# Attention over 16 groups: TensorE's program without its hardware loop, two key tiles of the row sums added elsewhere, four output buffers

## The chip, the cores and the metric

The kernel runs on one core of a Trainium2 chip. The metric is the device time of one execution in microseconds (us). Three executions of the kernel before took 3575.22, 3578.84 and 3588.54 us; the median is 3578.84 us. The profile comes from a further execution of its own.

## What is computed

The input x has 2 sequences of 2048 tokens with 1024 features. Cut to what matters:

```python
xn = layernorm(x)
q, k, v = xn @ wq, xn @ wk, xn @ wv      # 32 query heads, 8 key/value heads of 32 features
scores = where(causal, (q . k) * 32 ** -0.5, lowest)
s = (softmax(scores) @ v).reshape(b, s, 1024) @ wo
w = top-2-of-8 router weights of xn
g = silu(xn @ W_base.T + b_base + LoRA mixture of xn by w)
out = x + s * g
```

All operands are float32. The products are made exact enough by splitting a number into a rounded high part and the rest.

## The kernel before

The program has four parts, one after the other: project() makes q, k and v and stores them to DRAM, attend() does the attention, gate() makes g, output() multiplies by wo and finishes. The change touches attend() alone.

**Groups, chunks, tiles.** A group is one sequence with one key/value head and its NREP = 4 query heads; there are NG = 16 groups. A group has CPB = 4 chunks of CH = 512 queries, c = 0 to 3. Chunk c sees 4(c + 1) key tiles of 128 keys, j = 0, 1, .... For a pair of a key tile j and a block i of 128 queries TensorE makes one 128 x 512 tile of scores, keys by (head, query): that is operation T (line 1005, with line 1008 for the mask on the diagonal), 136 for a group, of which 10, 26, 42 and 58 belong to chunks 0 to 3. ScalarE takes the exponential of each (line 1043) into a buffer of 128 x 2048 for the whole key tile. The stretch from the first T of chunk c to the first T of the next chunk is called stage c here, and its start Sc.

**Row maxima ahead.** The shift for the softmax comes from scores in the other layout, queries by keys: TensorE makes pieces of rows (operation S, line 923, up to 512 keys), VectorE takes their maxima (lines 1067 and 1071), and operation M turns them into a row of the operand of T (lines 929, 1082, 817). These pieces run LEAD = 84 tiles ahead, so that those of the next group stand in this group's stages; four PSUM banks hold them.

**Values.** After each two key tiles of a chunk, operation W multiplies their exponentials by v, four matmuls per key tile (line 961). When the chunk is done, operation O on ScalarE copies the sum to o_sb (line 1057). There are two buffers o_sb, chosen by cc % 2.

**Row sums.** The softmax needs the sum of the exponentials over all keys. Three ways share this, by tables:

```python
ADDS = [[0, 1, 2, 3], [0, 3, 5, 6, 7], [0, 3, 5, 6, 8, 9, 10, 11], [0, 3, 5, 6, 8, 10, 12]]
DMA_ADDS = [[], [1, 2, 4], [1, 2, 4, 7], [1, 2, 4, 7, 9, 11]]
REST = [[], [], [], [13, 14, 15]]
```

The first tile of a list is the accumulator itself (buffers added and dma_added). GpSimd adds the other tiles of ADDS onto it (operation A, line 890). The others of DMA_ADDS are added by accumulating transfers of 1 MB, which GpSimd issues (operation D, line 900), each after the one before has landed. The tiles of REST are kept. Operation Y (line 978) is TensorE's: for each of added, dma_added and the tiles of REST it does four matmuls with a matrix of ones, and so waits until GpSimd's adds and the transfers of the chunk have ended. Y(c) stands nine tiles or so into the next stage; Y(3) in stage 0 of the next group.

**After the sums.** ScalarE copies Y's result to l_sb (line 1050, two buffers). Then L1 (line 860) moves a few rows of it to l_few, VectorE takes the reciprocal (operation I, line 1114), L2 (line 864) stores 8 KB to DRAM, L3 (line 868) spreads it back over l_sb in four transfers, GpSimd multiplies o_sb by l_sb (operation N, line 912), and L4 (line 873) stores o_sb and counts o_stored. L1 to L4 are issued by SyncE, whose queue is in order: L4(c) waits there for N(c).

**What sets the order.** stage(c) writes the operations in one list for all engines, by tile numbers: A(c,j), D(c,j), Y(c), N(c) and so on are the letters used below with chunk and key tile. Each engine goes through the lists in order. ScalarE's program is written out for all groups (over_stages_once, line 736); the others use over_stages (line 714), which has a hardware loop over pairs of groups (line 719), with three stages ahead of it and five behind:

```python
with engine.Fori(0, NPAIR - 1) as pair:
    for c in range(PEEL, CPB):
        run(Step(pair, 0), c, STAGES[c])
```

In both O(c) and Y(c) ScalarE waits for o_stored[cc % 2], that is, until the chunk two back has been multiplied and stored (lines 1049 and 1055). Of the 16 groups, groups 0 to 15, the loop's body goes from stage 3 of an even group to stage 2 of the next even one.

## Time and profile before

| what | value |
|---|---|
| runs | 3575.22, 3578.84, 3588.54 us |
| the profiled execution's own time | 3588.89 us |
| its span | 3587.1 us |
| mean granted TensorE clock | 0.957 |
| TensorE matmuls busy | 3328.6 us (93%) |
| VectorE busy | 1889.7 us (53%) |
| ScalarE busy | 1443.8 us (40%) |
| GpSimd busy | 1371.6 us (38%) |

The span is that from the first instruction to the last of the program; the profiled execution's own time is 1.8 us longer. Attention takes from about 709 to 2805 us of the span. The shares are averages over the four parts; what a wait is worth is read in attention itself. The granted clock is the share of 2.4 GHz at which TensorE ran; 0.50 is 1.2 GHz.

### The profile page before, as it was taken

What the parts mean: (1) busy time and instruction counts of PE and PEld (TensorE: products, weight loads), DVE (VectorE), ACT (ScalarE), POOL (GpSimd) and SP (SyncE); (2) the same over time, 40 slices, a digit from 0 to 9 for tenths busy, and PEclk for the clock granted to TensorE, in tenths of its full rate; (3) what the DMA queues carried; (4) which work ended last, traced back from release to release, by engine and by line L of the source; (5) the groups of instructions that cost most, each with busy time, mean ns of one, the idle gap of its engine ahead of it and who ended that gap; (6) DMA issues with size and microseconds to landing.
All of it is one profiled execution on the core that took longest, in us unless ns stands there. A gap on an engine that the chain in (4) does not pass through costs nothing. (4 is left out here: it accounts for less than half of the span.)

```text
span 3587.1 us, 59110 instructions
## 1 busy us (share of the span) xinstructions
PE 3328.6 (93%) x17920; PEld 2219.9 (62%) x17920; DVE 1889.7 (53%) x4622; ACT 1443.8 (40%) x2658; POOL 1371.6 (38%) x565
## 2 busy tenths in 40 slices
PE   6999999799989988989999998999999699999999
PEld 5888888554545544544554554554554488877887
DVE  5333332676666666766766666676673222223333
ACT  3122121165655555655655555565565210100100
POOL 0000000075665665766766675676577100000000
PEclk9999999699999999999999999999999899999999
DMA  6555544356556556656656655655565454435554
GB/s 223 160 163 180 160 153 135 89 125 130 128 122 135 126 119 138 135 122 133 141 119 136 135 125 121 139 130 121 130 153 130 138 172 137 133 126 190 193 190 172
DMA packets 285847, 511.84 MB, mean 143 GB/s; under 512 B 41120, under 2 KB 156832, under 8 KB 263584
## 3 DMA queue, kind: packets, MB, share of 16 engines
q1 hardware_dynamic: 260256, 333.04, 31.5%
q0 software_dynamic: 23040, 167.78, 23.2%
q10 hardware_dynamic: 2304, 7.87, 0.6%
q8 instruction: 137, 2.24, 0.3%
q14 instruction: 110, 0.90, 0.1%
HBM read 205.03 MB, written 134.74 MB: 95 GB/s over the span
## 5 line engine op out<-in xcount | busy, mean ns | idle before, releaser
L890 POOL TENSOR_TENSOR added<-added,probs 128x2048 f32<-128x2048 f32 (+3 forms) x320 | 1182.5, 3695 | 806.8 <-PE o_ps L961 772.5
L1067 DVE TENSOR_REDUCE row_max<-rows_ps 128x1 f32<-128x512 f32 x1536 | 996.3, 683 | 417.6 <-PE rows_ps L923 415.9
L1043 ACT ACTIVATE probs<-cols_ps 128x512 f32<-128x512 f32 x1728 | 921.7, 609 | 324.1 <-PE cols_ps L1005 296.9
L1071 DVE CUSTOM_DVE_ANT_0 masked_rows<-rows_ps,tri 128x128 bf16<-128x128 f32 (+3 forms) x1024 | 485.0, 482 | 228.3 <-PE rows_ps L923 225.3
L1005 PE MATMUL cols_ps<-q_st,k_st 97*128 97x512 f32 x1248 | 530.3, 432 | 54.7 <-ACT dma_added L1043 54.1
L923 PE MATMUL rows_ps<-k_st,q_st 96*128 96x512 f32 (+3 forms) x1536 | 536.5, 382 | 24.7 <-DMA q_st<-scratch_q_hi 16.9
L961 PE MATMUL o_ps<-probs,v_st 128*32 128x512 f32 (+3 forms) x4224 | 434.1, 528 | 0.0
L1005 PE MATMUL cols_ps<-q_st_last,k_st 97*128 97x512 f32 x928 | 388.7, 433 | 34.5 <-issue 30.3
L1005 PEld LDWEIGHTS cols_ps<-q_st,k_st 97*128 97x128 f32 x1248 | 242.0, 194 | 225.6 <-issue 106.9
L923 PE MATMUL rows_ps<-k_st,q_st_last 96*128 96x512 f32 (+3 forms) x1024 | 373.8, 390 | 1.9
L923 PEld LDWEIGHTS rows_ps<-k_st,q_st 96*128 96x128 f32 x1536 | 302.5, 198 | 116.9 <-DVE row_max L1067 49.2
L900 POOL DMA_DIRECT2D dma_added<-probs x160 | 139.9, 875 | 519.6 <-ACT probs L1043 448.0
L1005 PEld LDWEIGHTS cols_ps<-q_st_last,k_st 97*128 97x128 f32 x928 | 177.9, 192 | 188.4 <-issue 124.0
L438 PE MATMUL acc<-xt_hi,w_hi 128*128 128x512 f32 x704 | 281.6, 400 | 1.3 <-DVE logits L381 1.3
L440 PE MATMUL acc<-xt_hi,w_lo 128*128 128x512 f32 x704 | 277.6, 394 | 0.0
L439 PE MATMUL acc<-xt_lo,w_hi 128*128 128x512 f32 x704 | 276.8, 393 | 0.0
L1248 PE MATMUL g_acc<-gw_hi,g_t_hi 128*128 128x512 f32 x576 | 225.2, 391 | 22.0 <-DMA g_t_lo<-scratch_hw_lo 21.8
L961 PEld LDWEIGHTS o_ps<-probs,v_st 128*32 128x32 f32 x4224 | 112.5, 110 | 214.0 <-issue 145.2
L1043 ACT ACTIVATE added<-cols_ps 128x512 f32<-128x512 f32 x256 | 140.5, 598 | 239.0 <-PE cols_ps L1005 151.1
L923 PEld LDWEIGHTS rows_ps<-k_st,q_st_last 96*128 96x128 f32 x1024 | 200.5, 196 | 57.1 <-DVE row_max L1067 22.7
L395 DVE SCALAR_TENSOR_TENSOR out_lo<-acc,out_hi 128x512 fp32r<-128x512 f32 x80 | 55.3, 692 | 324.3 <-ACT out_hi L290 324.3
L1250 PE MATMUL g_acc<-gw_hi,g_t_lo 128*128 128x512 f32 x576 | 224.8, 390 | 0.0
(113 smaller groups left out, 3912.3 us busy)
## 6 DMA issues: line engine op xcount, KB each, us to landing
dma_added<-probs POOLq DMA_DIRECT2D x160, 1024.0 KB, 7.7
q_st<-scratch_q_hi SPq DMA_DIRECT2D x96, 256.0 KB, 6.9
x_sb<-in_x SPq DMA_DIRECT2D x32, 512.0 KB, 4.0
scratch_xt_hi<-xt_hi SPq DMA_DIRECT2D x32, 512.0 KB, 6.1
scratch_xt_lo<-xt_lo SPq DMA_DIRECT2D x32, 512.0 KB, 6.8
scratch_q_hi<-out_hi SPq DMA_DIRECT2D x64, 256.0 KB, 2.4
scratch_q_lo<-out_lo SPq DMA_DIRECT2D x64, 256.0 KB, 2.9
l_sb<-scratch_l_inv SPq DMA_DIRECT2D x256, 64.0 KB, 5.0
```

The costliest lines, as they stand in the source:

```text
L438: nc.tensor.matmul(out, lh, rh, start=(k == 0), stop=False)
L439: nc.tensor.matmul(out, lh, rl, start=False, stop=False)
L440: ins = nc.tensor.matmul(out, ll, rh, start=False, stop=(k == KT - 1))
L890: nc.gpsimd.tensor_tensor(total[:, :, q0:CH], total[:, :, q0:CH], probs_of(c, j)[:, :, q0:CH], ALU.add).then_inc(pool_added, 1)
L923: nc.tensor.matmul(rows_ps[rows_slot(k)][:, 0:keys], q_st[c][0:K1, h, i * P:(i + 1) * P], k_st[kbuf][0:K1, CH * p:CH * p + keys], start=Tr ...
L961: ins = nc.tensor.matmul(o_ps[h * HD:(h + 1) * HD, q0:CH], v_st[vbuf][:, j, :], probs_of(cc, j)[:, h, q0:CH], start=(j == 0), stop=(j == s ...
L1005: ins = nc.tensor.matmul(into, k_st[n.u][:, j * P:(j + 1) * P], q_st[c][:, :, i * P:(i + 1) * P], start=True, stop=not diagonal)
L1043: nc.scalar.activation(probs_of(c, j)[:, :, i * P:(i + 1) * P], cols_ps[cols_slot(AT_T[t])][:, :].rearrange("p (h q) -> p h q", h=NREP), A ...
L1067: nc.vector.tensor_reduce(into, bank[:, :], AX.X, ALU.max).then_inc(rows_free, 1)
L1071: nc.vector.tensor_tensor_reduce(masked_rows[rows_slot(k)][:, 0:keys], bank[:, 0:keys], tri[:, CH - keys:CH], 1.0, MASKED, ALU.add, ALU.ma ...
L1248: nc.tensor.matmul(acc[half][:, :], t_hi[u][:, k, :], w_hi[:, k, cols], start=(k == 0), stop=False)
L1250: return nc.tensor.matmul(acc[half][:, :], t_lo[u][:, k, :], w_hi[:, k, cols], start=False, stop=(k == NW - 1))
```

## The change

Three things are done.

- TensorE's attention program goes through over_stages_once, so its hardware loop is gone and all waits have constants. In the last group that function now leaves out the row pieces of a group after it, as over_stages did.
- In chunk 3 key tile 11 goes from the transfers to GpSimd (in the place of tile 12), and key tile 12 goes from GpSimd to REST, so that Y(3) has four matmuls more. DMA_ADDS of chunk 3 then has five tiles: the accumulator and four transfers onto it.
- There are four buffers o_sb and four counts o_stored, one for each chunk. O(c) waits until the same chunk of the group before has been stored. Y(c) waits for norm_ready instead, that is, until GpSimd's multiply of the chunk two back has read l_sb.

```diff
--- before.py
+++ after.py
@@ -544,10 +544,10 @@
 
 
 
-ADDS = [[0, 1, 2, 3], [0, 3, 5, 6, 7], [0, 3, 5, 6, 8, 9, 10, 11], [0, 3, 5, 6, 8, 10, 12]]
-DMA_ADDS = [[], [1, 2, 4], [1, 2, 4, 7], [1, 2, 4, 7, 9, 11]]
-
-REST = [[], [], [], [13, 14, 15]]
+ADDS = [[0, 1, 2, 3], [0, 3, 5, 6, 7], [0, 3, 5, 6, 8, 9, 10, 11], [0, 3, 5, 6, 8, 10, 11]]
+DMA_ADDS = [[], [1, 2, 4], [1, 2, 4, 7], [1, 2, 4, 7, 9]]
+
+REST = [[], [], [], [12, 13, 14, 15]]
 RING = [(c, j) for c in range(CPB) for j in range(TPC * (c + 1)) if j not in ADDS[c][:1] + DMA_ADDS[c][:1]]
 NRG = len(RING)
 
@@ -674,7 +674,7 @@
         masked_rows = [sb(f"masked_rows{i}", [P, CH], BF16) for i in range(NROWS)]
         shift = sb("shift", [P, NREP * TPC], FP32R)
         row = [sb(f"row{i}", [NREP * TPC, P]) for i in range(2)]
-        o_sb = [sb(f"o_sb{i}", [P, CH]) for i in range(2)]
+        o_sb = [sb(f"o_sb{i}", [P, CH]) for i in range(CPB)]
         l_sb = [sb(f"l_sb{i}", [P, CH]) for i in range(2)]
         l_few = [sb(f"l_few{i}", [P, NL]) for i in range(2)]
         l_inv = [sb(f"l_inv{i}", [P, NL]) for i in range(2)]
@@ -704,7 +704,7 @@
         l_inv_stored = [sem(f"a_l_inv_stored{i}") for i in range(2)]
         l_spread = [sem(f"a_l_spread{i}") for i in range(2)]
         norm_ready = sem("a_norm_ready")
-        o_stored = [sem(f"a_o_stored{i}") for i in range(2)]
+        o_stored = [sem(f"a_o_stored{i}") for i in range(CPB)]
         gw_loaded = sem("a_gw_loaded")
         NW = KT + 1
 
@@ -736,7 +736,8 @@
 
             for g in range(NG):
                 for c in range(CPB):
-                    run(Step(g // 2, g % 2), c, [op for op in STAGES[c] if not (g == 0 and of_group_before(op))])
+                    run(Step(g // 2, g % 2), c, [op for op in STAGES[c]
+                                                   if not (g == 0 and of_group_before(op) or g == NG - 1 and of_group_after(op))])
             for c in range(PEEL):
                 run(Step(NPAIR, 0), c, [op for op in STAGES[c] if of_group_before(op)])
 
@@ -871,10 +872,10 @@
                             wait_apart(sp, norm_ready, count, passed)
                             dst = sc["o"].rearrange("b g p c -> (b g) p c")
                             sp.dma_start(dst[bass.ds(n.lin(1, -back), 1), :, cc * CH:(cc + 1) * CH].squeeze(0),
-                                         o_sb[par][:, :]).then_inc(o_stored[par], 16)
+                                         o_sb[cc][:, :]).then_inc(o_stored[cc], 16)
             over_stages(sp, run)
-            for s in range(2):
-                sp.wait_ge(o_stored[s], 16 + 16 * (CPB * NG // 2))
+            for s in range(CPB):
+                sp.wait_ge(o_stored[s], 16 + 16 * NG)
             sp.wait_ge(gw_loaded, 16 * NW)
 
         @block.gpsimd
@@ -909,7 +910,7 @@
                         _, cc, back = op
                         wait_apart(pool, chunk_copied, n.lin(CPB, cc + 1 - CPB * back), passed_pool)
                         wait_apart(pool, l_spread[cc % 2], n.lin(32 * NREP, 16 * NREP * (cc // 2 + 1) - 32 * NREP * back), passed_pool)
-                        nc.gpsimd.tensor_tensor(o_sb[cc % 2][:, :], o_sb[cc % 2][:, :], l_sb[cc % 2][:, :], ALU.mult) \
+                        nc.gpsimd.tensor_tensor(o_sb[cc][:, :], o_sb[cc][:, :], l_sb[cc % 2][:, :], ALU.mult) \
                             .then_inc(norm_ready, 1)
             over_stages(pool, run)
 
@@ -1011,7 +1012,7 @@
                         weigh(n, *op[1:])
                     elif kind == "Y":
                         row_sums(n, *op[1:])
-            over_stages(pe, run)
+            over_stages_once(run)
 
         @block.scalar
         def _(act):
@@ -1046,15 +1047,17 @@
                     elif kind == "Y":
                         cc, back = op[1:3]
                         act.wait_ge(cols_full, cols_count(n, AT_Y[cc]))
-                        act.wait_ge(o_stored[cc % 2], n.lin(32, 16 * (cc // 2) + 16 - 32 * back))
+
+                        if cc >= 2 or not (first_group(n) or n.lin(1, -back) == 0):
+                            act.wait_ge(norm_ready, n.lin(CPB, cc - 1 - CPB * back))
                         nc.scalar.activation(l_sb[cc % 2][:, :], cols_ps[cols_slot(AT_Y[cc])][:, :], ACT.Copy) \
                             .then_inc(probs_ready, 1)
                     elif kind == "O":
                         cc, back = op[1:3]
 
-                        act.wait_ge(o_stored[cc % 2], n.lin(32, 16 * (cc // 2) + 16 - 32 * back))
+                        act.wait_ge(o_stored[cc], n.lin(16, 16 - 16 * back))
                         act.wait_ge(values_done, n.lin(NVG, J_OFF[cc + 1] // PER_VISIT - back * NVG))
-                        nc.scalar.activation(o_sb[cc % 2][:, :], o_ps[:, :], ACT.Copy).then_inc(chunk_copied, 1)
+                        nc.scalar.activation(o_sb[cc][:, :], o_ps[:, :], ACT.Copy).then_inc(chunk_copied, 1)
             over_stages_once(run)
 
         @block.vector
```

How the order moves, at the places that the prediction speaks of.

TensorE, at the end of the loop's body and just behind it (stage 2 turns into stage 3 there), before:

```order
L921 REGISTER_ALU
L923 MATMUL rows_ps<-k_st,q_st 128x384 [waits a_rows_free]
L921 REGISTER_ALU
L923 MATMUL rows_ps<-k_st,q_st 128x512 [waits a_rows_free]
L961 MATMUL o_ps<-probs,v_st 32x512 [waits a_probs_ready]
L961 MATMUL o_ps<-probs,v_st 32x512 x3
L961 MATMUL o_ps<-probs,v_st 32x384 x4
L719 REGISTER_ALU
L719 COMPARE_AND_BRANCH
L1005 MATMUL cols_ps<-q_st_last,k_st 128x512 [waits a_probs_ready,a_row_moved1]
L923 MATMUL rows_ps<-k_st,q_st 128x512 [waits a_rows_free]
L1005 MATMUL cols_ps<-q_st_last,k_st 128x512 [waits a_probs_ready]
```

The same place, between stages 2 and 3 of group 2, after the change:

```order
L924 MATMUL rows_ps<-k_st,q_st 128x384 [waits a_rows_free]
L924 MATMUL rows_ps<-k_st,q_st 128x512 [waits a_rows_free]
L962 MATMUL o_ps<-probs,v_st 32x512 [waits a_probs_ready]
L962 MATMUL o_ps<-probs,v_st 32x512 x3
L962 MATMUL o_ps<-probs,v_st 32x384 x4
L1006 MATMUL cols_ps<-q_st_last,k_st 128x512 [waits a_probs_ready,a_row_moved1]
L924 MATMUL rows_ps<-k_st,q_st 128x512 [waits a_rows_free]
L1006 MATMUL cols_ps<-q_st_last,k_st 128x512 [waits a_probs_ready]
```

The branch and the register operations are gone; the matmuls and their waits stand in the same order.

GpSimd, the end of its work for chunk 3 (the first row is A(3,8)), before:

```order
L890 TENSOR_TENSOR added<-added,probs 128x2048 [waits a_pool_added]
L67 REGISTER_ALU
L67 REGISTER_ALU [waits a_probs_ready]
L900 DMA dma_added<-probs 128x2048 [waits a_dma_done]
L885 REGISTER_ALU
L889 REGISTER_ALU [waits a_probs_ready]
L890 TENSOR_TENSOR added<-added,probs 128x2048 [waits a_pool_added]
L67 REGISTER_ALU
L67 REGISTER_ALU [waits a_probs_ready]
L900 DMA dma_added<-probs 128x2048 [waits a_dma_done]
L885 REGISTER_ALU
L889 REGISTER_ALU [waits a_probs_ready]
L890 TENSOR_TENSOR added<-added,probs 128x2048 [waits a_pool_added]
```

After the change:

```order
L891 TENSOR_TENSOR added<-added,probs 128x2048 [waits a_pool_added]
L67 REGISTER_ALU
L67 REGISTER_ALU [waits a_probs_ready]
L901 DMA dma_added<-probs 128x2048 [waits a_dma_done]
L886 REGISTER_ALU
L890 REGISTER_ALU [waits a_probs_ready]
L891 TENSOR_TENSOR added<-added,probs 128x2048 [waits a_pool_added]
L886 REGISTER_ALU
L890 REGISTER_ALU [waits a_probs_ready]
L891 TENSOR_TENSOR added<-added,probs 128x2048 [waits a_pool_added]
```

A(3,8), D(3,9), A(3,10), D(3,11), A(3,12) has become A(3,8), D(3,9), A(3,10), A(3,11).

ScalarE, O(3) (o_sb) and Y(3) (l_sb) of group 0, which stand in stage 0 of group 1, before:

```order
L1043 ACTIVATE added<-cols_ps 128x4x128 [waits a_cols_full] x4
L1043 ACTIVATE probs<-cols_ps 128x4x128 [waits a_pool_added,a_values_done,a_cols_full]
L1057 ACTIVATE o_sb<-o_ps 128x512 [waits a_values_done,a_o_stored1]
L1043 ACTIVATE probs<-cols_ps 128x4x128 [waits a_cols_full] x2
L1043 ACTIVATE probs<-cols_ps 128x4x128 [waits a_pool_added,a_values_done,a_cols_full]
L1043 ACTIVATE probs<-cols_ps 128x4x128 [waits a_cols_full]
L1043 ACTIVATE probs<-cols_ps 128x4x128 [waits a_dma_done,a_values_done,a_cols_full]
L1050 ACTIVATE l_sb<-cols_ps 128x512 [waits a_o_stored1,a_cols_full]
```

After the change:

```order
L1044 ACTIVATE added<-cols_ps 128x4x128 [waits a_cols_full] x4
L1044 ACTIVATE probs<-cols_ps 128x4x128 [waits a_pool_added,a_values_done,a_cols_full]
L1060 ACTIVATE o_sb<-o_ps 128x512 [waits a_values_done,a_o_stored3]
L1044 ACTIVATE probs<-cols_ps 128x4x128 [waits a_cols_full] x2
L1044 ACTIVATE probs<-cols_ps 128x4x128 [waits a_pool_added,a_values_done,a_cols_full]
L1044 ACTIVATE probs<-cols_ps 128x4x128 [waits a_cols_full]
L1044 ACTIVATE probs<-cols_ps 128x4x128 [waits a_dma_done,a_values_done,a_cols_full]
L1053 ACTIVATE l_sb<-cols_ps 128x512 [waits a_norm_ready,a_cols_full]
```

The rows stand where they stood. The copy to o_sb waits for the count of chunk 3 alone, where o_stored1 counted chunks 1 and 3 together, and the copy to l_sb for the multiply instead of a store. For O(1) both programs name o_stored1, but only in the first does it count chunk 3 too.

## Rows read from the trace of the kernel before

**Rows 1.** The page: engines, and TensorE's instruction fetches (packets, MB, share).

```profile
PE 3328.6 (93%) x17920; PEld 2219.9 (62%) x17920; DVE 1889.7 (53%) x4622; ACT 1443.8 (40%) x2658; POOL 1371.6 (38%) x565
...
q8 instruction: 137, 2.24, 0.3%
```

**Rows 2.** Waits of PE, 700 to 2900 us: us in total, times, longest.

```profile
PE cols_ps L1005 <- ACT dma_added L1043: 57.2, 31, 4.5
PE cols_ps L978 <- DMA dma_added<-probs: 55.6, 13, 5.4
PE cols_ps L1005 <- issue: 30.3, 6, 5.3
```

**Rows 3.** Timeline of PE: start, us, instruction [idle before it <- releaser].

```profile
1005.20 0.80 PE L1005 MATMUL cols_ps<-q_st,k_st 97*128 97x512 f32 x1 [3.55 <-ACT dma_added L1043]
...
1043.64 0.79 PE L1005 MATMUL cols_ps<-q_st_last,k_st 97*128 97x512 f32 x1 [4.93 <-issue]
...
1107.17 1.08 PE L978 MATMUL cols_ps<-added,ones 128*32 128x512 f32 x4 [4.58 <-DMA dma_added<-probs]
```

**Rows 4.** Stretches right behind waits: us, busy of each engine, PEclk, DMA share.

```profile
1005.20:1011.50 6.30, 6.30 (x26) 2.75 (x30) 1.95 (x4) 2.62 (x5) 1.06 (x1) 0.50 0.52 124
...
1107.20:1110.50 3.30, 3.30 (x16) 0.76 (x20) 0.00 (x0) 0.00 (x0) 2.69 (x2) 0.50 0.93 187
...
2755.80:2759.10 3.30, 3.30 (x15) 1.06 (x7) 0.00 (x0) 0.96 (x2) 0.00 (x0) 0.50 0.02 5
```

**Rows 5.** Timeline of PE, group 0: starts of stages 2, 3, Y(2), next group.

```profile
740.67 0.50 PE L1005 MATMUL cols_ps<-q_st,k_st 97*128 97x512 f32 x1
...
776.23 0.50 PE L1005 MATMUL cols_ps<-q_st_last,k_st 97*128 97x512 f32 x1
...
786.84 1.06 PE L978 MATMUL cols_ps<-added,ones 128*32 128x512 f32 x8 [1.90 <-POOL added L890]
...
825.97 0.50 PE L1005 MATMUL cols_ps<-q_st,k_st 97*128 97x512 f32 x1
```

**Rows 6.** Timeline of PE: starts of stages 0, 1 and 2 of group 3.

```profile
1093.69 0.50 PE L1005 MATMUL cols_ps<-q_st,k_st 97*128 97x512 f32 x1
...
1111.95 0.50 PE L1005 MATMUL cols_ps<-q_st,k_st 97*128 97x512 f32 x1
...
1133.51 0.50 PE L1005 MATMUL cols_ps<-q_st,k_st 97*128 97x512 f32 x1
```

**Rows 7.** Timeline of PE, group 15: its start, Y(2), Y(3).

```profile
2670.17 0.50 PE L1005 MATMUL cols_ps<-q_st,k_st 97*128 97x512 f32 x1
...
2755.01 1.27 PE L978 MATMUL cols_ps<-added,ones 128*32 128x512 f32 x8 [2.82 <-issue]
...
2799.71 1.93 PE L978 MATMUL cols_ps<-added,ones 128*32 128x512 f32 x8 [5.40 <-DMA dma_added<-probs]
```

**Rows 8.** Timeline of POOL, group 0: D(2,4), N(1), A(2,8) to A(2,11), D(3,11), A(3,12).

```profile
761.15 0.87 POOL L900 DMA_DIRECT2D dma_added<-probs  x1 [2.20 <-ACT probs L1043]
...
773.32 1.29 POOL L912 TENSOR_TENSOR o_sb<-o_sb,l_sb 128x512 f32<-128x512 f32 x1 [1.17 <-DMA l_sb<-scratch_l_inv]
774.58 12.13 POOL L890 TENSOR_TENSOR added<-added,probs 128x2048 f32<-128x2048 f32 x4
...
825.95 0.87 POOL L900 DMA_DIRECT2D dma_added<-probs  x1 [1.92 <-DMA dma_added<-probs]
826.56 4.90 POOL L890 TENSOR_TENSOR added<-added,probs 128x2048 f32<-128x2048 f32 x1
```

**Rows 9.** Timeline of POOL, stage 2 of group 3: N(0) and D(2,2).

```profile
1147.84 1.28 POOL L912 TENSOR_TENSOR o_sb<-o_sb,l_sb 128x512 f32<-128x512 f32 x1 [6.75 <-DMA l_sb<-scratch_l_inv]
1152.06 0.87 POOL L900 DMA_DIRECT2D dma_added<-probs  x1 [2.94 <-ACT probs L1043]
```

**Rows 10.** All instructions of line 900, the accumulating transfers of 1 MB.

```profile
DMA to landing us min/median/max: 6.8/7.7/14.0
```

**Rows 11.** Waits of SyncE's DMA queue: us in total, times, longest.

```profile
SPq L68 <- DMA scratch_l_inv<-l_inv: 113.8, 48, 7.2
```

## The prediction

> **What bounds the kernel now.** The page comes first. TensorE is busy 93% of the span, GpSimd 38% [rows 1], but GpSimd's work lies in attention alone. So attention's waits on TensorE are read next. Three releasers hold nearly all of them: a copy on ScalarE (57.2 us), the accumulating transfers in front of Y (55.6 us), and "issue", TensorE waiting for nothing but its own program (30.3 us, 6 times, one for each jump back of a loop with 7 passes) [rows 2]. The timeline shows one of each in groups 2 and 3: 3.55, 4.93 and 4.58 us [rows 3]. The first bears the name of dma_added because T stands behind it in ScalarE's queue, but what ScalarE waits for just ahead is the copy O(1), until o_sb of chunk 3 is stored.
>
> Each wait has an aftermath. Behind the wait of 3.55 us TensorE is granted 0.50 (1.2 GHz instead of 2.4) for 6.3 us with no idle time, behind that of 4.58 us for 3.3 us, and so it is behind one of only 2.82 us [rows 4, 7]. Work done at half the clock takes twice its time, so the aftermath costs half the stretch: 3.1 us behind O(1), about 1.7 behind Y(3); the branch is like the former, taken as 2.7.
>
> I cost the change not wait by wait but by stretches that I put together to a group, since a wait that goes may uncover the next one. The 14 groups 1 to 14 take 2670.17 - 825.97 = 1844.2 us, 131.7 each [rows 5, 7].
>
> **The pieces without the waits.** Stage 1 took 1133.51 - 1111.95 = 21.56 us with no wait inside [rows 6]. Stage 0 took 1111.95 - 1093.69 = 18.26; less its wait of 4.58 and 1.7 for the clock, 12.0 [rows 3, 4, 6]. Stage 2 of group 0 has neither an O(1) that waits nor a branch: 776.23 - 740.67 = 35.56 [rows 5]. From Y(2) to the next group it took 825.97 - 786.84 = 39.13 [rows 5].
>
> **Part 1, the loop goes.** The six waits on issue disappear, with 6 x (4.93 + 2.7) = 46 us at most. Stages 0 to 2 of group 0 and what follows the loop are already written out, and stage 2 there had no such wait [rows 5]; I cost the longer program at nothing. The register operations that go stood beside matmuls; nothing for them either. The page has 137 fetches for 35,840 instructions of TensorE [rows 1], so a block comes for each 262 of them, and the loop fetched its body anew in each pass: the traffic stays.
>
> **Part 2, tiles 11 and 12.** Y(3) gets four matmuls of 512 columns. Eight such took 1.06 us [rows 5], so 0.45 for the four, on TensorE's path, 7 us in all. D(3,11) goes. In group 0 it was issued at 825.95 [rows 8], when the next group began; now the last transfer is D(3,9), which had landed by then, since D(3,11) waited for it. So Y(3)'s last transfer has landed when the next group begins, nine tiles ahead of Y(3), and the wait of 4.58 goes with its 1.7. What is late next there? GpSimd: A(3,11) follows A(3,10) at once and takes 4.9 instead of A(3,12) (826.56 to 831.5 in group 0 [rows 8]). It needs neither tile 12 nor the transfer's issue, so it ends about 5 us sooner, and that was in time. Cost 0. GpSimd's adds stay 20 in number, its issues fall from 10 to 9 of 0.87 us. Tile 12's buffer now comes free at Y(3) only; its next user is key tile 6 of chunk 1, well into stage 1: nothing.
>
> **Part 3, four o_sb.** O(1) waits for a store a whole group old: its 3.55 us and 3.1 go. SyncE's queue is unchanged. Y(1)'s copy gets a wait for N(3), which by the table of events is due at tile 32 and Y(1) at tile 46: nothing, bounded above by the few us that O(1) waited for the same chain, one store further.
>
> **What becomes late: Y(2).** Stage 2 shrinks by 6.6 us, but GpSimd has the same work to do in it, and Y(2) needs A(2,11). In group 0, where O(1) did not wait, Y(2) had to wait 1.90 us for it [rows 5]. Group 0 is the mild case. There N(0) had no N(3) and no L4(3) ahead of it. In group 3 N(0) started at 14.3 us after S2 and ended at 15.6; D(2,2) was then not held up by it, since ScalarE's tile came later still, at 18.6 [rows 9]. With O(1)'s wait gone the tile comes 6.6 us sooner (12 us after S2) and N(0) becomes what holds D(2,2), at 15.6. It lands 6.8 to 7.7 us later [rows 10], so D(2,4) goes out at 23.0. In group 0 it took 774.58 + 12.13 - 761.15 = 25.6 us from D(2,4) to the end of A(2,11), of which 1.17 was a wait for l_sb [rows 8], which here is over before: 24.4. So A(2,11) ends 47.4 us after S2, where TensorE is ready for Y(2) at 786.84 - 1.90 - 740.67 = 44.3 [rows 5]. I forecast a wait of about 3 us at each Y(2), a new bound by GpSimd. The clock: behind 1.90 us no loss (eight matmuls took 1.06 there, the full speed), behind 2.82 half clock for 3.3 us [rows 4, 5]. The new wait is nearer to the second, so I take 1.0 of the 1.7.
>
> **The sum.** A group then takes 12.0 + 0.45 + 21.56 + 47.4 + 39.13 + 1.0 = 121.5 us. 14 groups: 1701, or 143 less. Group 0 had no wait that goes. Group 15: from its start to Y(2) it took 84.84 [rows 7], now 12.45 + 21.56 + 47.4 = 81.4, so 3.4 less; its Y(3) waited 5.40 us for D(3,11) and now waits for A(3,11) instead, 0 to 3 us less, I take 1.5. Together 148 us. The profiled execution's 3588.9 becomes 3441. It lies 10 us above the median of the three runs, a spread that has nothing to do with the change, so I give 3430 as the time.
>
> At one place a page speaks against my reading. SyncE waited 48 times, 113.8 us in all and up to 7.2, for a store of 8 KB [rows 11], as long as a transfer of 1 MB takes: small transfers issued behind a large one land with it. L2(1) will be issued 0.5 us after D(2,2) has landed, in a race with D(2,4); I take it to win. By that rule the sum stays 3430; by the rows, with the race lost, it is the third case below.
>
> **Other ways it could go.**
>
> *GpSimd keeps up as in group 0.* If N(0) comes sooner once stage 2 is quiet, Y(2) waits 1.9 us or less without a loss of clock. A group then takes 12.45 + 21.56 + 35.56 + (825.97 - 776.23 = 49.74) = 119.3 us [rows 5], 174 less over 14 groups, 179 in all: 3400. For it: group 0 is measured. Against it: N(0)'s place in group 3 is behind a chain that has nothing to do with O(1) [rows 9]. With no wait at all at Y(2) it would be 3372, but nothing shows that.
>
> *GpSimd is later still.* L2(1) loses the race, l_sb comes 1.2 us after N(1)'s turn, and each Y(2) pays the whole 1.7 of clock: 123.4 us, 117 less, 122 in all: 3457. L1(1) is now issued after D(2,2), so VectorE's reciprocal may wait some 2 us too, which the wait at Y(2) mostly takes in. For it: the long waits for 8 KB [rows 11].
>
> *The long program starves TensorE: slower.* Written out, it has 88 blocks of 262 instructions in attention (22,900 matmuls and weight loads). If the fetch of the next block were not under way, each would cost what the branch does, 7.6 us: 670 us, some 4100. It decides from 148 / 88 = 1.7 us a block. Against it: stage 2 of group 0 ran written out without such a wait [rows 5], as did the inside of the loop, where waits on issue came 6 times and no more [rows 2]. The Trainium skill ("Runtime: NRT & Kernel Launch", Instruction fetch mechanics) has the same two sides: blocks are prefetched in sequence, and a taken branch breaks that. By that rule this rival does not occur.
>
> *The change does not do what it says.* The order of instructions shows no branch and the new waits, so only part 3 could be void, if Y(1)'s new wait held ScalarE as O(1) did: 14 x 6.6 us less gain would partly come back from Y(2), and it would end near the 3457 of the third case. It is counted there.
>
> **Chances.** My forecast 0.52; as in group 0 0.20; later still 0.25; starved 0.03. The range leaves out the last and the ends of the outer two: 3392 to 3464. A measurement of this kernel tells 0.5%, 18 us, from no change, as its three runs span 13 us. All cases but the last are faster by 3% and more; 0.95 faster, 0.02 the same (a loss by fetches or GpSimd that eats just the gain), 0.03 slower.
>
> **What would show it.** In the profile after: no wait on issue at the top of stage 3 of the even groups; no wait at T in stage 2 behind O(1); none for dma_added at Y(3); instead waits at Y(2), about 3 us, released by GpSimd's add of chunk 2, in all groups; groups of about 121.5 us, stage 1 still 21.6; a mean clock above 0.957. D(2,2) some 15.6 us after S2. I am wrong if Y(3) still waits, if the waits at Y(2) are under 1.5 or over 5 us, or if waits on issue stand in straight code.

## The result and the profile after

| | before | after |
|---|---|---|
| median (lowest to highest), runs | 3580.36 us (3575.22 to 3588.54), 4 | 3470.14 us (3469.63 to 3474.85), 4 |
| the profiled execution, its span | 3588.89, 3587.1 us | 3470.59, 3468.8 us |
| mean granted TensorE clock | 0.957 | 0.972 |

The ratio is 0.9693, 95% interval [0.9672, 0.9714]: 110 us or 3.1% faster. The forecast was 3430 in a range up to 3464, so the sign is right and the gain too small: 148 us were promised on the profiled execution, 118 came.

The page of the changed kernel, lines that answer to [rows 1], and the granted clock in 40 slices:

```profile
PE 3313.3 (96%) x18048; PEld 2206.9 (64%) x18048; DVE 1887.7 (54%) x4622; ACT 1446.0 (42%) x2658; POOL 1357.8 (39%) x549
...
PEclk9999999789999999999999999999999899999999
...
q8 instruction: 113, 1.85, 0.2%
```

TensorE's waits, 690 to 2900 us (us in total, times, longest), answer to [rows 2]:

```profile
PE cols_ps L979 <- issue: 27.5, 13, 4.2
PE rows_ps L924 <- DVE row_max L1074: 22.9, 16, 4.1
```

All three of the old waits are gone. In their place stand the foreseen one at line 979 (at Y(2) in ten of the 16 groups, 23.9 of the 27.5 us, at Y(3) in group 15 alone), and one that was not foreseen: TensorE waits for VectorE's row maxima.

The waits at line 979 bear the name "issue", but in group 3 GpSimd's add of chunk 2 ends at 1142.68 + 12.22 = 1154.90, right where Y(2) starts. GpSimd's timeline in stage 2 of group 3, N(0), D(2,2), D(2,4) and the last adds, answers to [rows 8, 9]:

```profile
1121.54 1.28 POOL L913 TENSOR_TENSOR o_sb<-o_sb,l_sb 128x512 f32<-128x512 f32 x1 [6.87 <-DMA l_sb<-scratch_l_inv]
1122.76 0.88 POOL L901 DMA_DIRECT2D dma_added<-probs  x1
1130.71 0.88 POOL L901 DMA_DIRECT2D dma_added<-probs  x1 [2.45 <-DMA dma_added<-probs]
1142.68 12.22 POOL L891 TENSOR_TENSOR added<-added,probs 128x2048 f32<-128x2048 f32 x4
```

TensorE's timeline, the starts of stages 0 to 3 of group 3, its Y(2), and the start of group 4, answers to [rows 5, 6]:

```profile
1072.86 0.50 PE L1006 MATMUL cols_ps<-q_st,k_st 97*128 97x512 f32 x1
...
1085.56 0.50 PE L1006 MATMUL cols_ps<-q_st,k_st 97*128 97x512 f32 x1
...
1107.14 0.50 PE L1006 MATMUL cols_ps<-q_st,k_st 97*128 97x512 f32 x1
...
1144.41 0.50 PE L1006 MATMUL cols_ps<-q_st_last,k_st 97*128 97x512 f32 x1
...
1155.00 0.64 PE L979 MATMUL cols_ps<-added,ones 128*32 128x512 f32 x4 [1.87 <-issue]
...
1194.19 0.50 PE L1006 MATMUL cols_ps<-q_st,k_st 97*128 97x512 f32 x1
```

Term by term, group 3 is the forecast group:

| term | forecast | group 3 |
|---|---|---|
| stage 0 with the sums of tile 12 | 12.45 | 12.70 |
| stage 1 | 21.56 | 21.58 |
| D(2,2) behind S2 | 15.6 | 15.6 |
| S2 to Y(2) | 47.4 | 47.86 |
| Y(2) to the next group, with the clock's 1.0 | 40.13 | 39.19 |
| the group | 121.5 | 121.3 |

But the windows of groups 1 to 4 show that only every other group is like it (us, then busy us and instructions of PE, PEld, DVE, ACT, POOL, then the granted clock, DMA share, GB/s):

```profile
825.01:946.40 121.39, 117.74 (x729) 65.02 (x725) 88.97 (x236) 75.74 (x144) 85.96 (x34) 1.00 0.61 132
946.40:1072.86 126.46, 121.06 (x729) 66.90 (x725) 88.91 (x236) 76.39 (x144) 84.91 (x34) 0.96 0.59 126
1072.86:1194.19 121.33, 117.67 (x728) 64.99 (x724) 88.97 (x236) 75.76 (x144) 84.44 (x34) 1.00 0.61 132
1194.19:1321.05 126.86, 121.76 (x729) 66.95 (x725) 88.91 (x236) 76.40 (x144) 83.07 (x34) 0.96 0.58 126
```

The even groups take 5.2 us more, with a lower clock. The 14 groups 1 to 14 have a mean of (2559.96 - 825.01) / 14 = 123.9 us instead of 121.5. What the even groups have of their own is a jump: VectorE still goes through a hardware loop, and its jump back lies at the start of stage 3 of an even group, as TensorE's did. VectorE's timeline in group 2, the last instruction of its loop body and the first of the next pass:

```profile
1016.76 0.08 DVE L1074 DVE_READ_ACCUMULATOR2_ANT row_max<- 128x1 f32 x1
...
1023.94 0.69 DVE L1074 CUSTOM_DVE_ANT_0 masked_rows<-rows_ps,tri 128x512 bf16<-128x512 f32 x1 [7.09 <-issue]
```

TensorE there, and the stretch right behind its wait:

```profile
1024.69 1.41 PE L924 MATMUL rows_ps<-k_st,q_st 96*128 96x128 f32 x2 [4.05 <-DVE row_max L1074]
```

```profile
1024.70:1033.20 8.50, 8.36 (x27) 4.63 (x31) 5.73 (x19) 3.58 (x6) 2.56 (x2) 0.50 0.02 6
```

For 7.1 us VectorE has no instruction. The four banks of row pieces cover about three of them, then TensorE stands for 4.05 us, and behind that it is granted 0.50 (1.2 GHz) for 8.5 us. VectorE shows five such waits on issue, 32.7 us together, in groups 2, 4, 6, 10 and 12. In the kernel before there was the same loop with the same jump, but TensorE's own jump stood beside it, and VectorE was said to wait for TensorE. The same place in the kernel before:

```profile
1045.05 0.69 DVE L1071 CUSTOM_DVE_ANT_0 masked_rows<-rows_ps,tri 128x512 bf16<-128x512 f32 x1 [6.84 <-PE rows_ps L923]
```

From this row VectorE's jump can't be read, since the wait for TensorE alone is as long: with VectorE's loop written out and TensorE's kept, in an experiment below, the same place has

```profile
1036.45 0.69 DVE L1071 CUSTOM_DVE_ANT_0 masked_rows<-rows_ps,tri 128x512 bf16<-128x512 f32 x1 [6.55 <-PE rows_ps L923]
```

What the jump costs is shown by the experiments alone.

### The profile page after: what moved, and what is told of

It is laid out like the page before. It is cut to its first block and busy times, and to the rows that moved or that the text cites. A ratio compares the mean times of both kernels' runs of the same rounds, so it can differ in the third digit from the quotient of the medians.

```text
span 3468.8 us, 54971 instructions
## 1 busy us (share of the span) xinstructions
PE 3313.3 (96%) x18048; PEld 2206.9 (64%) x18048; DVE 1887.7 (54%) x4622; ACT 1446.0 (42%) x2658; POOL 1357.8 (39%) x549
## 5 line engine op out<-in xcount | busy, mean ns | idle before, releaser
L1006 PE MATMUL cols_ps<-q_st,k_st 97*128 97x512 f32 x1248 | 520.6, 424 | 0.6
L901 POOL DMA_DIRECT2D dma_added<-probs x144 | 125.6, 872 | 366.5 <-ACT probs L1044 320.0
L1252 PE MATMUL g_acc<-gw_lo,g_t_hi 128*128 128x512 f32 x576 | 224.8, 390 | 0.0
```

Source lines behind the costliest of these rows:

```text
L1006: ins = nc.tensor.matmul(into, k_st[n.u][:, j * P:(j + 1) * P], q_st[c][:, :, i * P:(i + 1) * P], start=True, stop=not diagonal)
L1252: nc.tensor.matmul(acc[half][:, :], t_hi[u][:, k, :], w_lo[:, k, cols], start=False, stop=False)
```

## The experiments

Diffs are against the changed kernel unless said otherwise. Times are medians, with the ratio to the kernel before and its interval. Kernels run on different chips are best compared by their ratios: the kernel before had medians of 3580.36, 3588.93, 3590.32 and 3582.10 us in the four sets of runs (first the result's, then the three of the experiments). The changed kernel ran in the first set only, so a difference from it is given by the medians and, where that tells another size, by the ratios too (1% is 36 us).

### VectorE's loop goes too

```diff
-            over_stages(dve, run)
+            over_stages_once(run)
```

> The changed kernel with VectorE's attention program written out too. Theory (VectorE's own jump back, 7 us without an instruction at stage 3 of the even groups, now stops TensorE, since TensorE no longer jumps at the same time): the even groups 2 to 12, at 123.6 to 128.8 us, fall to the 121.3 of the odd ones. Their excess over 121.3 adds to 5.2 + 5.6 + 6.4 + 2.3 + 4.7 + 7.5 = 32 us, so 3470 becomes about 3438; no wait for row_max over 1 us at stage 3. Rival (the excess comes from GpSimd's or SyncE's loop, or from the fetch of TensorE's long program): the excess stays and so does 3470.

3443.34 us, 0.9595 [0.9574, 0.9617]: 27 us less than the changed kernel by the medians, 35 by the ratios, the profiled execution 24.5 less (3446.1). TensorE's waits, 690 to 2700 us:

```profile
PE cols_ps L979 <- issue: 37.5, 19, 4.4
...
PE rows_ps L924 <- DVE row_max L1074: 3.1, 3, 1.7
```

The waits for row maxima are gone, the 14 groups have a mean of 121.9 us, and even groups are no longer than odd ones. The waits at Y(2) and Y(3) grew from 27.5 to 37.5 us in nearly the same window, so a part of what VectorE gave back was taken by GpSimd. Expected were 32 us less; the theory holds, with 24.5 to 35.

### Which loop costs what: the other three combinations

With TensorE's loop put back, parts 2 and 3 stand alone:

```diff
-            over_stages_once(run)
+            over_stages(pe, run)
```

> The changed kernel with TensorE back in its hardware loop (parts 2 and 3 alone). Theory (two jumps at the same place cover each other, so that taking one away gives only the difference): TensorE waits some 5 us on issue at stage 3 of six even groups with 2.7 of clock behind, 7.7 us, where it now loses about 5.3; some 12 to 15 us slower than the changed kernel, 3484, and VectorE's jump is hidden under it. Rival (the jump of TensorE is worth its full 46 us, as the prediction counted): 3516.

3481.57 us, 0.9698 [0.9676, 0.9720]: 11 us more than the changed kernel by the medians, 2 by the ratios. Taking out TensorE's jump alone is worth little here, since VectorE's takes its place.

The same with VectorE written out, so that TensorE's loop is the one that is left of the two:

> TensorE in its loop, VectorE written out, parts 2 and 3 as changed. Theory of the two jumps that cover each other: the same time as with both in loops, about 3484, within 5 us, since VectorE's jump had been under TensorE's. Rival (the two add up): 32 us less than with both in loops, about 3452.

3459.83 us, 0.9642 [0.9621, 0.9663]: 22 less than with both loops. I had expected that one jump covers the other in full; it doesn't. TensorE's waits at the top of stage 3, with both loops and with its own alone:

```profile
PE cols_ps L1006 <- issue: 32.4, 6, 6.5
```

```profile
PE cols_ps L1006 <- issue: 20.9, 6, 5.1
```

With both loops TensorE's waits at its jump are 5.4 us in the mean, with its own alone 3.5. On the kernel before this does not repeat (see below), so that one jump lengthens the other is not shown. The four times are 3481.6 with both loops, 3459.8 without VectorE's, 3470.1 without TensorE's, 3443.3 without either. Within one set of runs VectorE's loop costs 22 us beside TensorE's, and TensorE's 17 without VectorE's. The other two steps lead to the changed kernel, from another set: VectorE's loop alone costs 27 us by the medians and 35 by the ratios, TensorE's beside it 11 and 2.

GpSimd's loop, written out on top of VectorE's:

> VectorE and GpSimd written out as well as TensorE (3443 with VectorE's and TensorE's). Theory (GpSimd's jump falls on its idle time ahead of D(3,2), and its register operations between adds cost little): within 5 us of 3443. Rival (GpSimd is the engine that Y(2) waits for, and its loop lengthens its chain): 10 us or more faster, the waits at Y(2) shorter.

3446.68 us, 0.9604 [0.9573, 0.9635], 3 more than with VectorE's alone, within what can be told: GpSimd's jump costs nothing that these runs show.

### Part 2 undone: the tables of before

```diff
-ADDS = [[0, 1, 2, 3], [0, 3, 5, 6, 7], [0, 3, 5, 6, 8, 9, 10, 11], [0, 3, 5, 6, 8, 10, 11]]
-DMA_ADDS = [[], [1, 2, 4], [1, 2, 4, 7], [1, 2, 4, 7, 9]]
+ADDS = [[0, 1, 2, 3], [0, 3, 5, 6, 7], [0, 3, 5, 6, 8, 9, 10, 11], [0, 3, 5, 6, 8, 10, 12]]
+DMA_ADDS = [[], [1, 2, 4], [1, 2, 4, 7], [1, 2, 4, 7, 9, 11]]
-REST = [[], [], [], [12, 13, 14, 15]]
+REST = [[], [], [], [13, 14, 15]]
```

> The changed kernel with the old tables (part 2 undone). Theory (Y(3) waits for D(3,11) in most groups, 4.3 us and 1.7 of clock, against 0.45 for four matmuls more): 5.6 us for each of some 14 groups, 78 us slower than the changed kernel, 3548; waits for dma_added at the row sums of about 55 us again. Rival (with the other waits gone GpSimd issues D(3,11) early enough): within 20 us of 3470.

3485.08 us, 0.9717 [0.9696, 0.9737]: only 15 more (9 by the ratios), the rival's case; the theory's 78 did not come. TensorE's waits for the transfers at Y(3):

```profile
PE cols_ps L979 <- DMA dma_added<-probs: 21.1, 7, 7.3
```

D(3,11) is back, and yet the wait that held 55.6 us in [rows 2] holds 21.1. What goes with it is read below.

### Part 3 undone: two output buffers

```diff
-        o_sb = [sb(f"o_sb{i}", [P, CH]) for i in range(CPB)]
+        o_sb = [sb(f"o_sb{i}", [P, CH]) for i in range(2)]
...
-                        act.wait_ge(o_stored[cc], n.lin(16, 16 - 16 * back))
+                        act.wait_ge(o_stored[cc % 2], n.lin(32, 16 * (cc // 2) + 16 - 32 * back))
```

and so at every other place that part 3 touches.

> The changed kernel with two output buffers and the old waits for stores (part 3 undone). Theory (O(1) waits 3.5 us for the store of chunk 3 with 3.1 of clock behind; while it waits GpSimd catches up, so that the wait of 2 to 3 us at Y(2) goes): 6.6 us more in stage 2 and some 2.5 us less in stage 3 of each group, 4 us for 15 groups, 60 us slower than the changed kernel, 3530. Rival (the two waits stand side by side): 6.6 us a group, 3570. Rival (as with the tables, a wait that looked large is mostly taken over by others): within 30 us of 3470.

3506.73 us, 0.9767 [0.9735, 0.9798]: 37 more by the medians, between the theory's 60 and the second rival's 30, and 26 by the ratios, the second rival's case. The wait behind O(1) is back in full:

```profile
PE cols_ps L1006 <- ACT dma_added L1044: 60.2, 25, 5.1
```

The waits at Y(2) shrink to 0.3 to 1.9 us in the odd groups, as GpSimd has some 5 us longer, and the waits at line 979 from 27.5 to 12.2 us in all. TensorE's waits for the masked row maxima (line 1074, here 1072) shrink too, from 22.9 to 9.5. So part 3 removes 60 us of waiting with the half clock behind them, and pays part of it back at Y(2), as the prediction's sum had it, and part at VectorE, which it had not.

### One loop alone on the kernel before

Against the kernel before, with its filter for the last group:

```diff
-            over_stages(pe, run)
+            over_stages_once(run)
```

> The kernel before with TensorE written out and nothing else (part 1 alone). Theory (TensorE's jump goes, VectorE's at the same place is uncovered and costs 4 us of wait and half the clock behind it): some 12 us less than before, as on the new tables, 3578 where the kernel before takes 3590. Rival (the prediction's count of part 1): 46 us less, 3544.

3521.76 us, 0.9839 [0.9804, 0.9875]: 60 us less than before, more than either expectation (12 and 46). TensorE's waits:

```profile
PE cols_ps L1005 <- ACT dma_added L1043: 62.7, 25, 5.3
...
PE cols_ps L978 <- DMA dma_added<-probs: 15.8, 5, 7.2
PE rows_ps L923 <- DVE row_max L1071: 12.0, 10, 3.0
```

VectorE's jump shows up as it does in the changed kernel, though with only 12 us. What was not expected is the second line: the waits for D(3,11) fell from 55.6 to 15.8 us with no edit to the transfers.

The loop that was left, VectorE's, written out alone, and then both:

> The kernel before with VectorE written out and TensorE in its loop. With the tables of the change this was worth 22 us, because TensorE's own jump then took 2.9 to 5.1 us instead of 4.5 to 6.5. Theory (two jumps at a time lengthen each other): 10 to 22 us less than before. Rival (VectorE's jump lies under TensorE's and costs nothing): the same as before within 5 us.

> The kernel before with both written out. Theory (only with both gone is the jump gone): 40 to 46 us less than before, 3547, the count of the prediction for part 1. Rival (the waits at O(1) and Y(3) take in part of it): 25 us less or under.

VectorE's alone: 3586.73 us in 10 runs, 1.0013 [0.9997, 1.0030], no change, the rival's case. TensorE's jump is not shorter without VectorE's beside it, 4.9 us in the mean where [rows 2] has 30.3 us in six, 5.0:

```profile
PE cols_ps L1005 <- issue: 29.2, 6, 5.1
```

Both: 3495.88 us, 0.9755 [0.9721, 0.9790], 86 less, where 40 to 46 were expected. On the kernel before VectorE's loop costs nothing beside TensorE's, and 26 us (3521.8 to 3495.9) once TensorE's is gone. That is the clearest form of the finding. Why it cost 22 us beside TensorE's loop with the tables and buffers of the change is open.

### When the wait for D(3,11) comes, and what stays open

In the kernel before, Y(3) of a group waits 3 to 5 us or not at all. GpSimd issues D(3,11) near the start of the next group, and near it SyncE issues the load of q_st_last. Two places of the kernel before, the first at the start of group 4, with the wait of 4.52 us at Y(3), the second at that of group 6, without:

```profile
1222.62 0.34 SPq L798 DMA_DIRECT2D q_st_last<-scratch_q_hi  x1
...
1223.17 0.88 POOL L900 DMA_DIRECT2D dma_added<-probs  x1 [1.92 <-DMA dma_added<-probs]
```

```profile
1489.12 0.88 POOL L900 DMA_DIRECT2D dma_added<-probs  x1 [2.00 <-ACT probs L1043]
...
1490.43 0.34 SPq L798 DMA_DIRECT2D q_st_last<-scratch_q_hi  x1
```

The first landed 13.9 us behind its issue, the second 8.5. Five kernels have D(3,11): the one before, its three variants above and the one with the old tables. In all of them the order goes with the landing: issued ahead of the load the transfer lands in 8.4 to 10.4 us and Y(3) waits 0.35 us at most; behind it, in 9.8 to 14.0, and Y(3) waits 1.2 to 4.9. It was behind in 12 of 15 groups of the kernel before and in 3 with TensorE's loop out.

What decides the order is not TensorE's wait at Y(2). GpSimd issues D(3,2), the first of the chunk's transfers, 35.3 to 35.7 us ahead of the next group in every group of the five kernels, whether TensorE waited at Y(2) or not. What differs is the stretch from there to D(3,11), in which each transfer goes out after the one before has landed: in the kernel before 33.1 to 33.5 us in the three groups without the wait and 34.9 to 36.3 in the twelve with it. D(3,2) for the two places above:

```profile
1188.24 0.88 POOL L900 DMA_DIRECT2D dma_added<-probs  x1 [3.87 <-ACT probs L1043]
```

```profile
1456.06 0.88 POOL L900 DMA_DIRECT2D dma_added<-probs  x1 [3.87 <-ACT probs L1043]
```

To D(3,11) it takes 1223.17 - 1188.24 = 34.9 us in the first and 1489.12 - 1456.06 = 33.1 in the second; D(3,2) landed in 9.0 us there and 7.5 here. With TensorE's loop out D(3,2) landed in 6.8 to 7.3 us in ten of 15 groups, in the kernel before in one. Why it lands sooner then is open. That the load slows D(3,11), and doesn't only go with it, is not shown either: moving the load was not tried.

### What bounds the changed kernel, and a better version

With VectorE written out, the waits at Y(2) are what is left. Two tiles of chunk 2 move from GpSimd to TensorE:

```diff
-ADDS = [[0, 1, 2, 3], [0, 3, 5, 6, 7], [0, 3, 5, 6, 8, 9, 10, 11], [0, 3, 5, 6, 8, 10, 11]]
+ADDS = [[0, 1, 2, 3], [0, 3, 5, 6, 7], [0, 3, 5, 6, 8, 9], [0, 3, 5, 6, 8, 10, 11]]
-REST = [[], [], [], [12, 13, 14, 15]]
+REST = [[], [], [10, 11], [12, 13, 14, 15]]
...
-            over_stages(dve, run)
+            over_stages_once(run)
```

> VectorE written out and key tiles 10 and 11 of chunk 2 taken from GpSimd and summed by TensorE. Theory (GpSimd's last add of chunk 2 ends 2 to 3 us late, and these two adds take 2.5 and 1.3 us): no wait at Y(2), eight short matmuls more, 0.5 us; a group takes 118.6 us instead of 121.9, 46 us less, 3397. Rival (the wait turns into one for D(2,7) or for the next thing at the same place): at most 10 us less than 3443.

3406.13 us, 0.9493 [0.9462, 0.9525]: 37 less than with VectorE's loop out alone, where the theory had 46. The waits at Y(2) are gone, stage 3 takes 48.3 us instead of 49.9 and more. What is left is in stage 2, and VectorE's waits (820 to 2490 us) name it: the reciprocal waits for the little transfer L1(1), which is issued behind D(2,2) and lands with it.

```profile
DVE l_inv L1117 <- DMA l_few<-l_sb: 26.3, 23, 3.3
```

While VectorE stands there, its row maxima stand too. So the reciprocal of chunk 1 is put three tiles later:

```diff
-    event(_t + 12, "I", _c)
+    event(_t + (15 if _c == 1 else 12), "I", _c)
```

> As v7, with VectorE's reciprocal of chunk 1 three tiles later in its order. Theory (it stands 1 to 3.6 us at the reciprocal, since l_few lands only with D(2,2), and TensorE feels what four banks don't cover; stage 2 took 36.7 us in the mean instead of 35.6): no wait at the reciprocal, stage 2 at 35.6, 10 to 16 us less than v7, 3385. Rival (the banks cover it, and the excess of stage 2 comes from elsewhere, or the later reciprocal makes l_sb late for N(1)): the same as v7 within 5 us, or slower.

3389.94 us (3389.47 to 3390.28), 0.9444 [0.9413, 0.9474]: 16 less again. VectorE's waits for L1, and group 11 as a window:

```profile
DVE l_inv L1117 <- DMA l_few<-l_sb: 9.2, 18, 2.0
```

```profile
2013.70:2131.80 118.10, 116.81 (x745) 65.98 (x741) 88.37 (x236) 75.44 (x144) 81.46 (x32) 1.00 0.62 135
```

TensorE is busy in 116.8 of the 118.1 us of this group, at the full clock. This version beats both kernels, by 5.6% and by 2.3% (2.6% by the ratios).

The later reciprocal on the changed kernel by itself:

> The changed kernel with VectorE's reciprocal of chunk 1 three tiles later. It was worth 16 us where Y(2) did not wait. Theory (what TensorE loses to VectorE in stage 2 is taken in by the wait at Y(2), whose end GpSimd sets): within 5 us of 3470. Rival (it adds): 10 to 16 us less.

3466.28 us, 0.9677 [0.9644, 0.9710], 4 less. Stage 2 shrinks to 35.6 us, but the waits at Y(2) grow to 2.4 to 4.8 us in the groups that have one: GpSimd's chain ends when it ends, and what TensorE gains ahead of it is lost there. The prediction had said so of this wait.

## Why the prediction was right and wrong

**What fell away: right.** No wait on issue for TensorE at the top of stage 3, none behind O(1) that counts (2.1 us in ten of line 1006), none at Y(3) of groups 0 to 14 for a transfer. The copy Y(1) with its new wait costs nothing: groups with no VectorE jump come out near the sum, 120.2 to 121.6 us in five of the seven odd ones.

**What becomes late, Y(2): right in place, and near in size.** In group 3 D(2,2) goes out 15.6 us behind S2 as forecast (14.3 to 16.3 in groups 1 to 15), the add's end 47.8 instead of 47.4, the wait 1.8 to 2.2 us instead of 3 in most odd groups, 3.8 and 4.2 in groups 9 and 13. In the even groups with a jump TensorE's wait for VectorE comes just ahead of Y(2) and takes it in; with VectorE's loop out the wait stands in every group but group 8, at 2.0 to 4.4 us. It is smaller than forecast because stage 2 takes 36.2 to 37.6 us rather than group 0's 35.56. Those are the microseconds for which VectorE's reciprocal waits for L1(1) (26.8 us in 22 waits between 900 and 2600 us):

```profile
1130.28 0.25 DVE L1117 RECIPROCAL l_inv<-l_few 128x16 f32<-128x16 f32 x1 [2.26 <-DMA l_few<-l_sb]
```

The third case of the prediction foresaw this and said that the wait at Y(2) takes it in; the later reciprocal by itself (4 us) shows that it does. L1(1) was issued 0.9 us behind D(2,2):

```profile
1123.62 0.61 SPq L861 DMA_DIRECT2D l_few<-l_sb  x1
```

**The clock: right at Y(2) of group 3, but no rule.** Behind 1.87 us at Y(2) the granted clock stays 1.00, as I had read from [rows 5], so that the 1.0 us of the sum was not paid there:

```profile
1155.10:1158.50 3.40, 3.40 (x24) 1.66 (x24) 0.84 (x3) 1.52 (x4) 0.00 (x0) 1.00 0.02 5
```

But in stage 2 of group 8 a wait of only 0.76 us for row maxima (at 1750.70) was followed by 6.7 us at 0.50 (1.2 GHz) with no idle time to speak of:

```profile
1753.50:1760.20 6.70, 6.64 (x27) 2.83 (x25) 3.62 (x15) 2.75 (x5) 6.62 (x3) 0.50 0.58 119
```

The same happened behind 1.08 us in group 12. The length of the wait just ahead doesn't tell by itself whether the clock falls.

**The step that failed is part 1, "the loop goes".** I counted TensorE's jumps and their aftermath and called the stage 3 behind them free, because stage 2 and 3 of group 0 ran so. But group 0 had no jump of any engine. VectorE's loop ends at the same place, its jump takes 7 us, and in the kernel before it lay under TensorE's, where it cost nothing. Uncovered, it costs 5.8 us in group 2 (stage 3 took 55.58 us against 49.79 in group 3) and 27 us in the kernel (24.5 between the profiled executions). Without it the profiled execution is 3446.1 against my sum of 3441. The Trainium skill ("Runtime: NRT & Kernel Launch", Instruction fetch mechanics) says that a taken branch breaks the prefetch of an engine's instructions. I used it against the rival of a starved TensorE, where it held: no wait in straight code. Applied to every engine that kept its loop, it would have named VectorE, and GpSimd too, whose jump cost nothing; what it costs at VectorE no row of before shows apart.

**The base was wrong by 10 us.** The profiled execution of before lay above its median, and I took 10 us off the sum for that. The changed kernel's profiled execution is at its own median (3470.59 and 3470.14). In 13 runs the kernel before spread over 23 us (3570.85 to 3594.13), the changed one over 5 in its four, the best version over 1. Of these three only the first has the wait at Y(3) that comes or stays away by group; that it is what spreads the runs is argued, not shown. Against it stands the kernel with the old tables, which has such a wait of over 1 us in five of 15 groups and spread over 5 us in its four runs. Whatever made the one execution slow did not come along with the change. These two, 24.5 for the jump and 10 for the base, are most of the 40 us by which 3430 missed; the remaining 5 are about what is seen in stage 2 of groups 8 and 12 (40.0 and 40.7 us, the two places above where the clock falls). One small term was short as well: the sums of tile 12 were put at 0.45 us a group, and stage 0 grew by 0.86, from 11.85 in the groups of before that did not wait to 12.71.

**The parts are no terms of a sum.** Undoing part 1, 2 or 3 costs 11, 15 and 37 us by the medians, 63 together (37 by the ratios), where the whole gives 110; part 1 alone gives 60 on the kernel before, where I wrote "46 us at most". The limit was false since with the jump the waits for D(3,11) went from 55.6 to 15.8 us too. The sum still came out within 5 us apart from VectorE, because it was made of stretches up to the next bound and not of the waits that go. In part that is luck: in group 3 the 1.0 us for the clock that was not paid makes up for the terms that came out longer.

**"The traffic stays" was wrong, harmlessly.** TensorE's program, written out, was fetched in 113 blocks, in its loop in 137 [rows 1] and 142: the loop fetched more, not the same.

**The rivals.** GpSimd keeping up (3400) did not come. The starved TensorE did not come either; stage 1, written out in all groups, has 21.56 to 21.59 us everywhere. The case "later still" (3457) is the nearest in number, but for another reason: the race of L2 against D(2,4) was won (in group 3 by 0.1 us, and N(1) did not wait), and the time went at VectorE.

## What to carry to other kernels

When one engine's loop is written out, list every engine whose loop jumps at the same place; a jump that lies beside another's shows no cost of its own, and has one when the other is gone (here 0 us before, 26 once TensorE's loop was out). Cost a change by stretches up to the next point where two engines meet, and not by the waits that go: a wait that is gone sets free a later one, and another can go with it. And where an execution lies above the median, ask which wait makes it so, and whether the change leaves it there, before the difference is carried over.

## What was not expected of the hardware

- The engines' jumps differ. VectorE stood 6.8 to 7.1 us in four of its five, TensorE 2.1 to 6.5. With the tables of the change TensorE's took 5.4 us in the mean beside VectorE's and 3.5 without it, on the kernel before 5.0 and 4.9. GpSimd's cost nothing that the runs show. SyncE's program was not written out.
- Half the clock for 6.7 us came behind a wait of 0.76 us, and none behind one of 1.87 us.
- The accumulating transfer D(3,11) of 1 MB landed 8.4 to 10.4 us after its issue where it went out ahead of the load of q_st_last, and 9.8 to 14.0 where it went out behind it. That one causes the other was not tried.
- A wait of TensorE for GpSimd's add can stand under "issue" in the waits (nearly all of 27.5 us here); in group 3 the add ended 0.1 us ahead of the matmul.
